# Feed-forward 0 of a fused decoder: transposing the requantised gelu tile by DMA instead of on TensorE

## The reference, cut to what matters

```python
def quant(x):                       # per row, per 128 columns
    amax = max(abs(x), over the 128 columns)
    scale = maximum(amax, 0.0001) / 448
    return float8_e4m3(x / scale) * scale
...
X = layernorm(x).astype(bfloat16)                    # (2048, 512)
D = gelu(quant(X) @ quant(W0).T + bias0).astype(bfloat16)   # (2048, 1792)
x = x + (quant(D) @ quant(W1).T + bias1).astype(bfloat16)   # (2048, 512)
```

## Time and profile before

| | us |
|---|---|
| median of three runs (1837.88 to 1840.01) | 1839.16 |
| the profiled execution | 1841.43 |
| its span | 1838.90 |
| busy: PE / DVE / ACT / POOL | 1642.4 / 1316.7 / 785.6 / 326.4 |
| feed-forward 0, from its first transposition of x to its last addition to X | 1054.7 to 1437.7 |

### The profile page before, as it was taken

The page is one execution under the profiler, slowest core; times in us unless marked ns, Lnnn a source line. Parts: engine busy times, 40 slices in busy tenths (PEclk is TensorE's granted clock), DMA queues, the critical chain, the costliest instruction groups (busy, mean ns, idle before and its releaser), DMA issues. The chain is left out here.

```text
span 1838.9 us, 30560 instructions
## 1 busy us (share of the span) xinstructions
PE 1642.4 (89%) x11334; PEld 903.3 (49%) x11334; DVE 1316.7 (72%) x2451; ACT 785.6 (43%) x1692; POOL 326.4 (18%) x266
## 2 busy tenths in 40 slices
PE   4899999999999999999999679999997796888793
PEld 3455555555555555555555234455554354555441
DVE  6567666776676667766758578988877536999688
ACT  3424242434242424342424256666765323555451
POOL 2001000010010000100100111111110224777414
PEclk9899999999999999999999889999999898999897
DMA  6121311212213112122113110000002001000002
GB/s 240 24 70 24 81 47 36 70 35 58 70 24 81 47 36 70 35 58 70 24 35 104 22 71 1 1 1 0 0 0 58 1 0 35 0 0 0 0 1 91
DMA packets 109247, 74.47 MB, mean 40 GB/s; under 512 B 69202, under 2 KB 90963, under 8 KB 108884
## 3 DMA queue, kind: packets, MB, share of 16 engines
q1 hardware_dynamic: 79428, 39.86, 8.3%
q10 hardware_dynamic: 29712, 33.03, 5.6%
HBM read 44.57 MB, written 11.53 MB: 31 GB/s over the span
## 5 line engine op out<-in xcount | busy, mean ns | idle before, releaser
L520 PE MATMUL pj<-XT,WQ 128*128 128x512 f16 x1536 | 343.5, 380 | 18.9 <-DVE QT L714 12.5
L562 PE MATMUL xp<-WO,OT 128*128 128x512 f16 x1536 | 339.7, 381 | 1.8 <-DVE X L813 1.8
L520 PEld LDWEIGHTS pj<-XT,WQ 128*128 128x128 f16 x1536 | 145.5, 98 | 202.3 <-DVE QT L714 31.0
L562 PEld LDWEIGHTS xp<-WO,OT 128*128 128x128 f16 x1536 | 148.1, 98 | 184.6 <-issue 13.2
L655 ACT ACTIVATE E<-E 128x512 f32<-128x512 f32 x64 | 40.4, 632 | 380.2 <-DVE E L750 380.2
L500 POOL TENSOR_TENSOR VW<-VW,XB 128x1024 f32<-128x1024 f32 x14 | 33.0, 2356 | 797.6 <-DVE VW L107 797.6
L813 DVE SCALAR_TENSOR_TENSOR X<-xp,X 128x512 f32<-128x512 f32 x128 | 88.3, 691 | 119.9 <-PE xp L562 118.9
L920 PE MATMUL db<-W0T,XD 128*128 128x448 f16 x768 | 161.0, 361 | 0.0
L946 PE MATMUL eb<-W1T,DT 128*128 128x512 f16 x672 | 150.1, 383 | 0.9 <-DVE DT L1096 0.9
L714 DVE SCALAR_TENSOR_TENSOR QT<-pj,QT 128x512 f16<-128x512 f32 x128 | 87.9, 687 | 80.2 <-ACT QT L638 78.4
L638 ACT ACTIVATE QT<-pj 128x512 f16<-128x512 f32 x128 | 75.7, 591 | 115.4 <-PE pj L520 115.4
(11 more groups left out here) (225 smaller groups left out, 2727.5 us busy)
## 6 DMA issues: line engine op xcount, KB each, us to landing
W0T<-in_L_xattn_wq ACTq DMA_DIRECT2D x7, 1024.0 KB, 5.4
W0T<-in_L_xattn_wo ACTq DMA_DIRECT2D x7, 1024.0 KB, 5.0
CS<-in_ctx SPq DMA_DIRECT2D x4, 1024.0 KB, 10.1
X<-in_x SPq DMA_DIRECT2D x4, 1024.0 KB, 11.2
out<-X SPq DMA_DIRECT2D x16, 256.0 KB, 2.0
XB<-in_L_ffn_W ACTq DMA_DIRECT2D x14, 256.0 KB, 2.9
w0t<-XB ACTq DMA_DIRECT2D x7, 512.0 KB, 3.3
w1t<-W0T ACTq DMA_DIRECT2D x7, 512.0 KB, 3.8
```

The source lines that it names most:

```text
L520: last = pe.matmul(bank[:, :], w, src[:, b, k, tokens], start=n == 0, stop=n == 3 * KC - 1)
L562: last = pe.matmul(xp[i % 2][:, :], OT[:, a, j, i * P:(i + 1) * P], WO[:, b, j, :], start=n == 0, stop=n == 3 * REP - 1)
```

## The change

- `et`, `transpose_hidden`, `high_e` and `low_e` go. In their place the tile is split where it lies, in SBUF: ScalarE writes the high part in two halves (`high_d`), VectorE the low part in two halves (`low_d`), both into `HL`, which is the memory of `MD` seen as float16. SyncE transposes each part, 128 by 1792, into `DT` by a DMA of its own: high when both high halves are there and the second product of the tile before has ended (`e_done`), then low when both low halves are there. Each DMA adds 16 to `dt_done`.
- VectorE's `grid_d` does its first operation (L100), then waits for both transposes of the tile before, since the next one (L102) writes `MD`.
- TensorE's step is: four banks of the first product, transposition of x, second product, which waits for both transposes once.
- x's subtraction moves from GpSimd to VectorE (`off_grid_x`); `quant_x` on VectorE is in two parts, the first between the two maxima of gelu. GpSimd keeps the multiplication (`dequantise_x`), and its step begins with a wait for `dm_done` of the hidden tile, VectorE's multiplication L105 on `MD`.
- The order of ScalarE's step changes: x's multiplication first, then three gelus, half of the scaling, the fourth gelu, and so on. Attention 1's weights are loaded behind the last transposes in SyncE's queue.

```diff
         MD = sb(ph, "MD", [P, IC, P], F32)
+        HL = MD[:, :, :].rearrange("p c t -> p (c t)").bitcast(F16).rearrange("p (s c t) -> p s c t", s=2, c=IC)
-        et = [pb(ph, f"et{i}") for i in range(2)]
...
+            def step(i):
+                hidden = ahead(i, -1)
+                if live(hidden):
+                    if live(ahead(hidden, -1)):
+                        sp.wait_ge(S["e_done"], count(hidden, 1, 0))
+                    sp.wait_ge(S["dh_done"], count(hidden, 2, 2))
+                    sp.dma_start_transpose(DT[:, 0, :, :], HL[:, 0, :, :].rearrange("p c t -> p (c t)")).then_inc(S["dt_done"], 16)
+                    sp.wait_ge(S["dl_done"], count(hidden, 2, 2))
+                    sp.dma_start_transpose(DT[:, 1, :, :], HL[:, 1, :, :].rearrange("p c t -> p (c t)")).then_inc(S["dt_done"], 16)
+
+            for i in range(TILES + 1):
+                step((0, i))
             sp.wait_ge(S["d_done"], 4 * TILES)
             load_weights1(sp)
...
-            def transpose_hidden(i, n):
-                pe.wait_ge(S["dqs_done"], count(i, 4, n + 1))
-                if n >= 2 or live(ahead(i, -1)):
-                    pe.wait_ge(S["et_lo"], count(i, 4, n - 1))
-                for c in range(*GROUP_OF[n]):
-                    last = pe.transpose(et[n % 2][:, (c % 4) * P:(c % 4 + 1) * P], VD[:, i[1] % 2, c, :], ident[:, :])
-                last.then_inc(S["et_done"], 1)
...
-                for n in range(4):
-                    pe.wait_ge(S["et_lo"], count(i, 4, n + 1))
-                    for c in range(*GROUP_OF[n]):
-                        for a, b in PASSES:
-                            last = pe.matmul(eb[:, :], DT[:, a, c, :], W1T[:, b, c, :],
-                                             start=False, stop=c == IC - 1 and (a, b) == PASSES[-1])
+                pe.wait_ge(S["dt_done"], count(i, 32, 32))
+                for c in range(IC):
+                    for a, b in PASSES:
+                        last = pe.matmul(eb[:, :], DT[:, a, c, :], W1T[:, b, c, :],
+                                         start=False, stop=c == IC - 1 and (a, b) == PASSES[-1])
                 last.then_inc(S["e_done"], 1)
             def step(i):
                 old, nxt = ahead(i, -2), ahead(i, 1)
-                if live(old):
-                    transpose_hidden(old, 0)
-                    transpose_hidden(old, 1)
                 if live(i):
-                    first_product(i, (0, 1, 2))
-                if live(old):
-                    transpose_hidden(old, 2)
-                    transpose_hidden(old, 3)
+                    first_product(i, range(4))
                 if live(nxt):
                     transpose_x(nxt)
-                if live(i):
-                    first_product(i, (3,))
                 if live(old):
                     second_product(old)
...
@@ -991,20 +982,22 @@
                 r = i[1] % 2
                 act.wait_ge(S["dstep"], count(i, SCALE_STEPS, SCALE_STEPS))
                 if live(ahead(i, -2)):
-                    act.wait_ge(S["et_done"], count(i, 4, -4))
+                    act.wait_ge(S["dl_done"], count(i, 2, -2))
...
+                act.wait_ge(S["dq_done"], count(i, 2, n + 1))
+                for c in range(*HALVES[n]):
+                    last = act.activation(VD[:, r, c, :], VD[:, r, c, :], ACT.Copy, scale=ds_[:, r, c:c + 1])
+                last.then_inc(S["dqs_done"], 1)
+
+            def high_d(i, n):
+                a, b = HALVES[n]
+                act.wait_ge(S["dqs_done"], count(i, 2, n + 1))
+                act.activation(HL[:, 0, a:b, :], VD[:, i[1] % 2, a:b, :], ACT.Copy).then_inc(S["dh_done"], 1)
...
+                older, hidden, nxt, after = (ahead(i, by) for by in (-3, -1, 1, 2))
                 if live(older):
                     out_e(older)
-                if live(old):
-                    high_e(old, (0, 1))
-                if live(i):
-                    gelu(i, (0, 1, 2))
-                if live(old):
-                    high_e(old, (2, 3))
-                if live(nxt):
-                    high_x(nxt)
                 if live(after):
                     x_times_rec(after)
                 if live(i):
+                    gelu(i, (0, 1, 2))
+                if live(hidden):
+                    d_times_scale(hidden, 0)
+                if live(i):
                     gelu(i, (3,))
+                if live(nxt):
+                    high_x(nxt)
                 if live(hidden):
-                    d_times_scale(hidden, range(4))
+                    high_d(hidden, 0)
+                    d_times_scale(hidden, 1)
+                    high_d(hidden, 1)
                 if live(i):
                     d_times_rec(i)
...
+            def off_grid_x(i):
+                dve.wait_ge(S["xsum"], count(i, 1, 1))
+                dve.tensor_tensor(VX[:, :, :], VX[:, :, :], MX[:, :, :], ALU.subtract).then_inc(S["xq_done"], 1)
...
             def grid_d(i):
-                to_grid(dve, VD[:, i[1] % 2, :, :], MD[:, :, :],
-                        [S[n] for n in ("dw_done", "dcut", "dbits", "dm_done", "dsum")], count(i, 1, 1))
+                sems = [S[n] for n in ("dw_done", "dcut", "dbits", "dm_done", "dsum")]
+                to_grid(dve, VD[:, i[1] % 2, :, :], MD[:, :, :], sems, count(i, 1, 1), (0, 1))
+                if live(ahead(i, -1)):
+                    dve.wait_ge(S["dt_done"], count(i, 32, 0))
+                to_grid(dve, VD[:, i[1] % 2, :, :], MD[:, :, :], sems, count(i, 1, 1), (1, 4))
...
+            def low_d(i, n):
+                a, b = HALVES[n]
+                if n == 0:
+                    dve.wait_ge(S["dq_done"], count(i, 2, 2))
+                dve.wait_ge(S["dh_done"], count(i, 2, n + 1))
+                dve.tensor_tensor(HL[:, 1, a:b, :], VD[:, i[1] % 2, a:b, :], HL[:, 0, a:b, :],
+                                  ALU.subtract).then_inc(S["dl_done"], 1)
...
             def step(i):
-                old, hidden, nxt, after = (ahead(i, by) for by in (-2, -1, 1, 2))
-                if live(old):
-                    low_e(old, (0, 1))
+                hidden, nxt, after = (ahead(i, by) for by in (-1, 1, 2))
                 if live(hidden):
                     grid_d(hidden)
                     off_grid_d(hidden)
                 if live(i):
                     amax_d(i, 0)
-                if live(old):
-                    low_e(old, (2, 3))
+                if live(after):
+                    quant_x(after, (0, 2))
+                if live(i):
+                    amax_d(i, 1)
                 if live(nxt):
                     low_x(nxt)
                 if live(i):
-                    amax_d(i, 1)
                     scales_d(i)
+                if live(hidden):
+                    low_d(hidden, 0)
+                    low_d(hidden, 1)
                 if live(after):
-                    quant_x(after)
+                    quant_x(after, (2, 4))
+                    off_grid_x(after)
...
-            def quant_x(i):
-                V, M = VX[:, :, :], MX[:, :, :]
-                pool.wait_ge(S["xsum"], count(i, 1, 1))
-                pool.tensor_tensor(V, V, M, ALU.subtract).then_inc(S["xq_done"], 1)
+            def dequantise_x(i):
                 if live(ahead(i, -1)):
                     pool.wait_ge(S["xt_lo"], count(i, 1, 0))
                 pool.wait_ge(S["xq_done"], count(i, 1, 1))
-                pool.tensor_tensor(QX[:, :, :], V, xs[:, nr(i), :].unsqueeze(2).to_broadcast([P, KC, P]),
+                pool.tensor_tensor(QX[:, :, :], VX[:, :, :], xs[:, nr(i), :].unsqueeze(2).to_broadcast([P, KC, P]),
                                    ALU.mult).then_inc(S["xqs_done"], 1)
...
             def step(i):
-                older, nxt = (ahead(i, by) for by in (-3, 1))
+                older, hidden, nxt = (ahead(i, by) for by in (-3, -1, 1))
+                if live(hidden):
+                    pool.wait_ge(S["dm_done"], count(hidden, 1, 1))
                 if live(nxt) and fixed(nxt) != 0:
-                    quant_x(nxt)
+                    dequantise_x(nxt)
                 if live(older):
                     add_x(older)
```

More of the change, by code:

```diff
@@ L865, in ffn0 @@
                  "xt_done xt_hi xt_lo d_done ones_done bias_zeroed bias_ready gelu_done da_done dstep dw_done dcut dbits dm_done dsum "
-                 "dq_done dqs_done et_done et_hi et_lo e_done eb_done x_done")
+                 "dq_done dqs_done dh_done dl_done dt_done e_done eb_done x_done")
         S = {n: sem(ph, "f0_" + n) for n in names.split()} | x_sems
@@ L997, in d_times_rec, with d_times_scale @@
                 last.then_inc(S["dw_done"], 1)
-            def d_times_scale(i, ns):
+            def d_times_scale(i, n):
                 r = i[1] % 2
[L1001 to L1007, removed]
+                act.wait_ge(S["dq_done"], count(i, 2, n + 1))
[6 more added lines that the diff above has]
+                act.activation(HL[:, 0, a:b, :], VD[:, i[1] % 2, a:b, :], ACT.Copy).then_inc(S["dh_done"], 1)
```

(29 more changed lines are left out.)

4 lines of the change are left out of this document (removed).

## The result

The changed kernel takes 1861.66 us (median of four, 1857.8 to 1863.63), the kernel before beside it 1838.52 (its median of four here): a ratio of 1.0123, with a 95% interval of 1.0105 to 1.0142. It is 23.1 us slower. The profiled execution took 1861.57 with a span of 1859.8 (20.9 more than before); TensorE was busy for 1618.6, VectorE for 1340.8, ScalarE for 783.0, GpSimd for 344.3. TensorE has 23.8 us less to do, and the kernel is longer.

A forecast was written before the change was run, and what follows sets the result against it. TensorE was taken to set the 21.08 us pass. Passes +9, x's last quarter +3, fill +3.8, clock +6.4 and drain 0 made +22 on 1839.2: 1861 us, range 1836 to 1880.

The forecast's parts named there:

- GpSimd is held behind L107: After L105: VectorE's L107 goes first, GpSimd's 1.04 us multiplication of x is held and ends at 5.3, not 3.4.
- rival 2: After L105: GpSimd comes first, L107 is stretched by about 0.9; pass 20.3 us, total 1837; chance 0.07.
- The first way round the ring: Chain of waits from one transpose landing to the next, through GpSimd, ScalarE, VectorE and the transfer: 21.8 us.
- The landing of 4.3: SyncE's DMA transposes of 128x1792: issue 2.1, data 1.7, tail 0.5, so 4.3 us; 3.5 and 5.1 kept as bounds.
- The estimate of 3.05: The same DMA transposes by the skill's formula, 2.0 us plus bytes over 436 GB/s: 3.05 us; not adopted.
- A pass +0.75: Each pass of feed-forward 0's tile loop: 21.8 us against 21.08, so +0.75; twelve passes give +9.
- The clock, 8 x 0.8: TensorE's second products after idling 2.5 us: lower clock in 8 passes at 0.8 us, +6.4; 0 and 13 kept.
- The five early passes: First passes of feed-forward 0: x's last quarter, normalised in passes 1 to 4, adds net +3 to pass and clock costs.
- The fill, +3.8: Before the first second product: chain from L105 of tile 0 at 1085.7 makes it start at 1116.3, not 1112.5.
- The drain, 0: End of feed-forward 0: it loses its transposes and gains transfers, net 0.

The follow-up runs named there:

- e1: The changed kernel without GpSimd's wait for VectorE's multiplication (L105) of the hidden tile: 1828.58 us, ratio 0.9950.
- e8: The changed kernel, but VectorE's addition L107 waits until GpSimd has multiplied x, so GpSimd goes first: 1852.0 us, ratio 1.0081.
- e2: The changed kernel with GpSimd's wait moved from L105 to the end of VectorE's addition L107: 1888.32 us, ratio 1.0271.
- e9: The changed kernel with the pieces of x's last layernorm quarter in VectorE's steps 2, 4, 5, 6 and 8: 1859.96 us, ratio 1.0117.
- e7: The changed kernel with the layernorm statistics behind feed-forward 0 taken one step later: 1858.88 us, ratio 1.0117.

## Why the prediction was right, and where only its sum was

The forecast was 1861 and the time is 1861.66; the mechanism is the one it named, and the size of its terms is less good than the sum. That the sum came within 1 us is luck.

- *GpSimd is held behind L107.* Right: 2.71 and not 1.04, ending 5.2 after the landing (5.3 was forecast). VectorE's pair takes 1.7 more (0.7 + 0.9 was forecast). e1 shows that the wait is the cause, e8 that the hold follows the order and not the instruction. The Trainium skill (SBUF — State Buffer, Who interferes with whom) has this rule, with the order of issue as what decides; the 2.71, 2.96 and 1.70 of these traces agree. What the hold by itself costs a pass, apart from the wait that ties x's chain to gelu's tile, no run isolates. e8 comes nearest: with the multiplication first, the pass was 21.24 and the time 1852, and not the 20.3 and 1837 of rival 2, though there L107 also waits 1.40 for GpSimd, which the rival's order would not need.
- *The first way round the ring.* Right nearly step by step: x's multiplication ends at 6.6 (forecast 6.6), the half of the scaling at 9.95 (10.05), the low halves at 17.2 (17.5), the landing at 21.36 (21.8).
- *The landing of 4.3.* Measured 4.15, in other parts: the issue is 1.5 to 1.7 and did not grow with the blocks as assumed (2.1), the data take longer, 2.1 and not 1.7. This window is the low part's data, with the rate at its end; L478's moved at 238:

```profile
1296.80:1298.90 2.10, 2.10 (x13) 1.08 (x11) 1.35 (x2) 1.17 (x4) 0.00 (x0) 1.00 1.14 213
```

The estimate of 3.05 from the Trainium skill (DMA: Bandwidth & Descriptors, Anatomy of one DMA), whose figures are for another queue kind, disagrees with the measured 4.0 to 4.2.
- *A pass +0.75.* Mis-sized: +0.28 in the steady passes. 0.3 of the difference is the low halves, which ended sooner, and 0.15 the landing.
- *The clock, 8 x 0.8.* Mis-sized in its place: the steady passes, whose stall is 1.59 and not 2.5, lose nothing. The early ones do lose: after a stall of 2.73 the transposition of x ran at 0.50, and the five second products took 10.29, 10.14, 11.26, 9.23 and 11.59, 6.4 over five times 9.23. In e2, stalls of 2.7 to 2.8 bring the clock down in every steady pass. The length of the stall alone doesn't decide, though: the changed kernel's 2.58 before 1391.09 and e9's 3.31 were both followed by a second product of 9.23. The first two rows are of the changed kernel, TensorE's timeline and a window, the next two the same of e9:

```profile
1143.99 1.12 PE L939 MATMUL xt<-ident,VW 128*128 128x128 f32 x4 [2.73 <-POOL VW L1136]
```

```profile
1143.80:1147.20 3.40, 2.99 (x9) 1.76 (x11) 3.40 (x3) 3.23 (x10) 2.10 (x2) 0.51 0.00 0
```

```profile
1188.41 0.66 PE L939 MATMUL xt<-ident,VW 128*128 128x128 f32 x4 [3.31 <-POOL VW L1136]
```

```profile
1188.40:1191.80 3.40, 3.38 (x18) 1.83 (x19) 2.87 (x2) 3.37 (x7) 1.92 (x1) 1.00 0.00 0
```

- *The five early passes.* By the prediction's terms they were 5 x 0.75 + 3 + 5 x 0.8 = 10.75, if five of its eight clock passes are laid here; measured 10.0. How much of the 6.4 above lengthened these passes was not measured, since TensorE waits in each of them anyway, so the split between x's work and the clock stays open.
- *The fill, +3.8.* The step that failed: measured +8.4. 2.3 of it came before the point from which the sum began: VectorE's L105 of tile 0 ended at 1088.0 and not at the 1085.7 taken from the earlier trace rows. 1.8 of that was there already at the second maximum of tile 0 (1073.06, before 1071.23), 0.5 of it the later start of the stage: in the new order VectorE's low part of x stands behind two steps of the next tile's grid, and the first product began 1.3 later. The other 0.5 came right behind that maximum, where the low part of x now stands in front of the scale steps. The rest lies in the chain after L105, which was 33.1 long and not 30.6 (its written terms add up to 30.35). Two terms of it can be named. Before the first gelu of tile 1 ScalarE loads a function table, 1.28, which the prediction put at nothing: it stands right behind x's multiplication, and that waits for GpSimd, so the load is on the chain, while without the wait (e1) it is over by 1085.3. And the transposition of x before the second product took 1.33 with its issue and not 0.5; after a stall of 8.82 it ran at the lower clock. The same load stands behind x's multiplication once more at 1170.30, in an early pass. First VectorE's timeline of the changed kernel, then ScalarE's and TensorE's, then ScalarE's of e1:

```profile
1058.16 0.40 DVE L100 TENSOR_SCALAR VW<-VW 128x512 uint32<-128x512 uint32 x1
1058.59 0.43 DVE L102 TENSOR_SCALAR VW<-VW 128x512 uint32<-128x512 uint32 x1
1058.93 0.68 DVE L1083 TENSOR_TENSOR XD<-xt,XD 128x512 f16<-128x512 f32 x1
...
1086.93 1.09 DVE L105 TENSOR_SCALAR MD<-MD 128x1792 f32<-128x1792 f32 x1
```

```profile
1091.02 1.28 ACT L978 ACTIVATE VW<-XB,xrec 128x128 f32<-128x128 bf16 x4 [7.45 <-POOL VW L1136]
1092.31 1.28 ACT L1005 ACT_TABLE_LOAD   x1
```

```profile
1119.81 1.11 PE L939 MATMUL xt<-ident,VW 128*128 128x128 f32 x4 [8.82 <-POOL VW L1136]
```

```profile
1083.97 1.28 ACT L1005 ACT_TABLE_LOAD   x1
```

- *The drain, 0.* Failed too: +1.7; the copy of `eb` that e7 frees is worth 2.7 of the last gaps. The prediction followed transposes and transfers there, and not ScalarE's queue.

So the seven later passes were forecast at 7 x 0.75 + 3 x 0.8 = 7.65 and cost 3.0, fill and drain were forecast at 3.8 + 0 and cost 10.1; these errors, -4.7 and +6.3, and the -0.75 of the early passes nearly cancel. The time alone would not have shown it.

## What to carry to other kernels

A wait that releases GpSimd at the same instant as the next two-operand instruction of VectorE bought nothing here: VectorE's instruction went first, and every engine behind GpSimd was late by the rest of it (2.71 for 1.04). Release GpSimd where VectorE waits anyway, here under the transfer (33 us between the two places). Look also at what a wait ties together: x's chain ran one tile ahead on its own before, and here the wait put it into the ring of gelu's tile; fill and first passes pay for that more than a steady pass shows. And look at what stands in a queue behind the instruction that now waits: here ScalarE's table load of 1.28 moved from idle time onto the chain.

## What the runs showed of the hardware

- VectorE's instructions with one source are held as well, and hold: in e1, beside GpSimd's two operations, L100 took 1.67 and L102 1.86 in place of 1.09 in the pass shown (medians 1.35 and 1.16), and GpSimd's addition 2.00 in place of 1.16. The prediction had thought of those with two operands. The shown duration includes the hold: GpSimd's 1.04 was shown as up to 2.88 behind an instruction of 2.03 and as 1.70 behind one of 1.09.
- Released by the same event, VectorE went on after 0.03 and GpSimd after 0.25.
- A DMA transposition of 128x1792 float16 was issued in 1.52 and landed in 4.0 at the least, one of 128x1024 in 1.23 and 2.8: with 1.75 times the data the issue grew by a quarter and the landing by 43%.
- Each load of a function table on ScalarE took 1.28 in feed-forward 0 of both kernels.
